# Delta rule in a four-stage fp32 kernel: keys multiply the state in the recurrence, the inverse's levels roll over the chunks, and the gate projections stand behind the inverse

## The chip, the cores and the metric

The kernel runs on one core of one Trainium2 chip. The metric is the device time of one execution in microseconds (us). All arithmetic is fp32.

## What is computed

Four layers follow each other over `BATCH = 8` sequences of `SEQ = 512` tokens with `DIM = 256` features: a gated mixer, a mixture of experts, a delta-rule attention and a token-selecting attention. The change is in the third one alone. Its reference, cut to what matters (8 heads, keys of 128, values of 64):

```
q = _causal_dw_conv_silu(x @ Wq, conv_q).reshape(bsz, seq_len, H, KD)
k = _causal_dw_conv_silu(x @ Wk, conv_k).reshape(bsz, seq_len, H, KD)
v = _causal_dw_conv_silu(x @ Wv, conv_v).reshape(bsz, seq_len, H, VD)
q = _l2norm(q)
k = _l2norm(k)
def step(state, inp):
    q_t, k_t, v_t, a_t, b_t = inp
    retained = jnp.einsum('bhvk,bhk->bhv', state, k_t)
    ...
    state = a4 * (state - b4 * rk) + b4 * vk
    o_t = jnp.einsum('bhvk,bhk->bhv', state, q_t)
    return (state, o_t)
...
gate = (x @ Wg).reshape(bsz, seq_len, H, VD)
rms = jax.lax.rsqrt(jnp.mean(out * out, axis=-1, keepdims=True) + EPS_RMS)
out = out * rms * o_norm_w * jax.nn.silu(gate)
return out.reshape(bsz, seq_len, VAL_DIM) @ Wo
```

The kernel computes the recurrence in `NC = 4` chunks of `C = 128` tokens. Within a chunk the dependence of each token on the earlier ones is a triangular matrix for each head; its inverse (`XT`) times the scaled values gives what each token adds to the state, and the state is carried from chunk to chunk.

## The kernel before

`stage_delta` writes the instructions of each engine out by hand; semaphores tie the engines together and no scheduler moves anything. Each engine has a function `body(pb, b)` that handles the front part of batch `b` (projections, convolutions, inverse, tail) and the recurrence and output of batch `pb = b - 1`. `body(None, 0)` and the last `body(7, None)` are written out; the seven between them are one hardware loop (`Fori`), so that every engine jumps back at its end.

One body goes through these parts, in this order on the tensor engine (PE):

- **K projections**: eight times `proj` (L1378, two 128x512 matmuls each). ScalarE copies each out (`cp`), multiplies it by a tap (`tap`), VectorE adds the three other taps (`conv(n)`, L1735: three instructions of 128x512), and ScalarE applies silu (`step`). There are 20 such convolutions in a batch: 0 to 7 keys, 8 to 11 values, 12 to 19 queries.
- **scan** of batch `pb`: four chunks; each multiplies the inverse by the values (L1392), a matrix `WT` by the state (L1396), the queries by the state (L1402), the keys by `Ud` for the next state (L1407) and `PQ` by `U` for the output (L1411). Each of these is a group of eight matmuls, one for each head. VectorE does `decay_state`, `decay_u`, `new_state`, `out_a` and `out_b` between the key convolutions and eight scans of the decays (`decay`, L1765).
- **gram**: the keys times themselves (L1422, four groups), multiplied by the decays on VectorE (`DG`, L1812); V projections; transposes of the keys (L1431); Q projections and the four gate projections (L1382).
- On VectorE alone meanwhile: 13 small instructions on the query norms, squares and sums of the output (L1820, L1821), the normalisation that ends in `yf`, and then the **base of the inverse** (L1838 to L1858), a chain of over 60 dependent instructions that inverts 32x32 blocks.
- **project_out** of batch `pb` (L1442, L1447) and on VectorE the residual add (L1863, `outr`), for which PE waits before the next part.
- **invert**: levels y5 (L1463), x5 (L1469), x11 (L1480), y6 (L1485), x6 (L1492) and then w (L1500), which multiplies the inverse by scaled keys into `WT`; all six for chunks 0 and 1, and then all six for chunks 2 and 3. VectorE scales y5 and y6 out of PSUM (L1872, L1880) and does the twelve convolutions 8 to 19 between them.
- **tail**: transposes of the values (L1509, scaled on VectorE at L1892, `values`), and four times the product of keys and queries (L1518) followed by sums of squared queries (L1523). The first L1518 waits until all 20 convolutions are through.

SyncE's queue loads weights, `hT`, decays (`ab`) and the residual input (`xin`, one body ahead), and stores the result.

## Time and profile before

| | us |
|---|---|
| median of three runs | 3805.78 |
| lowest and highest of them | 3804.8 and 3806.32 |
| the profiled execution, its own time | 3808.81 |
| its span, first to last instruction | 3806.2 |
| of it the delta stage, first K projection to its last store | 1713.2 to 3284.6 |
| of it the seven bodies of the loop | 1876.9 to 3187.7 |

Over the whole span PE is busy 86%, VectorE (DVE) 63%, ScalarE (ACT) 36%. PE's granted clock is shown as a share of 2.4 GHz: 0.50 is 1.2 GHz. In the delta stage no engine is busy all the time: the parts above follow each other, and in each another engine is the one that the others wait for.

### The profile page before, as it was taken

To read this page: it belongs to the slowest core of one execution; us is meant where nothing else is said; L and a number is where in the kernel's file an instruction comes from. 1 tells how busy PE (TensorE), PEld (TensorE's weight loads), DVE (VectorE), ACT (ScalarE), POOL (GpSimd) and SP (SyncE) were. 2 spreads that over 40 slices of the span, in tenths; PEclk is the share of its full clock that TensorE was granted. 3 is DMA by queue.
4 is the path that set the end of the run, shared out by engine and by line. 5 is a ranking of instruction groups with operands and counts; after the bars stand their busy time and mean duration, and the time that the engine had idled before them with its cause. 6 is when DMAs were issued, how large, how long until landed. Compare 5 with 4: busy or idle time off the path is not lost. (4 is left out here: it accounts for less than half of the span.)

```text
span 3806.2 us, 52445 instructions
## 1 busy us (share of the span) xinstructions
PE 3262.9 (86%) x18666; PEld 2525.1 (66%) x18666; DVE 2396.6 (63%) x5801; ACT 1356.5 (36%) x2713; POOL 158.4 (4%) x158
## 2 busy tenths in 40 slices
PE   5999938888999999747989898989898989488887
PEld 2665524445999999714867686868686869355554
DVE  6788425554777777766685858576767673354542
ACT  2333202221444444314534444444444442033232
POOL 0000000015111111000000000000000000000000
PEclk8999958999999999968797988888888886588786
DMA  1000080022899989741011111110111100100000
GB/s 62 23 17 12 11 160 12 11 75 81 305 322 317 320 318 323 253 152 64 34 34 35 34 36 34 35 34 35 34 35 34 35 20 1 53 12 23 12 17 12
DMA packets 203686, 327.31 MB, mean 86 GB/s; under 512 B 37449, under 2 KB 157522, under 8 KB 202258
## 3 DMA queue, kind: packets, MB, share of 16 engines
q1 hardware_dynamic: 196930, 305.94, 24.4%
q0 software_dynamic: 6480, 17.77, 1.2%
q8 instruction: 164, 2.69, 0.3%
q14 instruction: 112, 0.92, 0.1%
...
## 5 line engine op out<-in xcount | busy, mean ns | idle before, releaser
L767 PE MATMUL ex_ps<-ex_xbT,ex_w 128*128 128x128 f32 x4544 | 531.2, 275 | 1.7 <-DMA ex_b<-in_b_all_dram 1.2
L767 PEld LDWEIGHTS ex_ps<-ex_xbT,ex_w 128*128 128x128 f32 x4544 | 524.3, 192 | 6.1 <-DMA ex_b<-in_b_all_dram 1.8
L1378 PE MATMUL de_ps<-de_hT,de_w 128*128 128x512 f32 x640 | 306.2, 636 | 27.6 <-DMA de_w<-in_w_kqv_dram 13.9
L896 ACT ACTIVATE ex_t<-ex_ps,ex_b 128x128 f32<-128x128 f32 x568 | 208.8, 368 | 337.0 <-PE ex_ps L767 319.1
L1378 PEld LDWEIGHTS de_ps<-de_hT,de_w 128*128 128x128 f32 x640 | 129.0, 207 | 188.1 <-issue 186.0
L711 PE MATMUL ex_ps<-ex_xT,ex_w 128*128 128x512 f32 x512 | 230.6, 607 | 12.5 <-DVE ex_gl L1008 9.1
L1008 DVE SCALAR_TENSOR_TENSOR ex_gl<-ex_ps,ex_b,ex_t 128x128 f32<-128x128 f32 (+1 forms) x316 | 123.7, 391 | 137.3 <-ACT ex_t L896 69.4
L711 PEld LDWEIGHTS ex_ps<-ex_xT,ex_w 128*128 128x128 f32 x512 | 98.0, 195 | 131.8 <-issue 115.0
L1735 DVE SCALAR_TENSOR_TENSOR de_ya<-de_kx,de_taps,de_ya 128x512 f32<-128x512 f32 x192 | 142.5, 751 | 49.2 <-ACT de_ya L1574 44.7
L1008 DVE SCALAR_TENSOR_TENSOR ex_gm<-ex_ps,ex_b,ex_t 128x128 f32<-128x128 f32 (+1 forms) x316 | 121.8, 385 | 48.9 <-ACT ex_t L869 46.6
L177 PE MATMUL mx_ps<-mx_hT,mx_w_in 128*128 128x512 f32 x320 | 143.6, 605 | 8.3 <-ACT mx_hT L249 8.3
L1735 DVE SCALAR_TENSOR_TENSOR de_ya<-de_qx,de_taps,de_ya 128x512 f32<-128x512 f32 x192 | 142.9, 751 | 8.7 <-ACT de_ya L1574 2.6
L779 PE MATMUL ex_ps<-ex_w,ex_hid 128*128 128x256 f32 x568 | 134.5, 380 | 1.8 <-DVE ex_hid L1033 1.8
L1485 PE MATMUL de_ps<-de_PQ,de_DG 64*128 64x64 f32 x512 | 113.4, 419 | 15.7 <-ACT de_PQ L1638 15.7
L1485 PEld LDWEIGHTS de_ps<-de_PQ,de_DG 64*128 64x128 f32 x512 | 110.4, 329 | 19.6 <-ACT de_PQ L1638 19.6
L869 ACT ACTIVATE ex_t<-ex_ps,ex_b 128x512 f32<-128x512 f32 x64 | 44.0, 687 | 207.3 <-PE ex_ps L711 207.3
L177 PEld LDWEIGHTS mx_ps<-mx_hT,mx_w_in 128*128 128x128 f32 x320 | 60.7, 193 | 81.6 <-issue 67.4
L211 PE MATMUL mx_ps<-mx_h2T,mx_w_fc 128*128 128x512 f32 x256 | 113.7, 603 | 0.8 <-ACT mx_h2T L271 0.8
L1030 DVE SCALAR_TENSOR_TENSOR ex_gl<-ex_gl,ex_gm 128x128 f32<-128x128 f32 (+1 forms) x316 | 105.4, 333 | 11.1 <-DVE ex_gl L1028 0.2
L1033 DVE TENSOR_TENSOR ex_hid<-ex_gl,ex_gs 128x128 f32<-128x128 f32 (+1 forms) x316 | 105.0, 332 | 11.2 <-DVE ex_gl L1030 0.2
L220 PE MATMUL mx_ps<-mx_w_proj,mx_hid 128*128 128x256 f32 x512 | 111.8, 379 | 0.0
L779 PEld LDWEIGHTS ex_ps<-ex_w,ex_hid 128*128 128x128 f32 x568 | 102.5, 190 | 12.9 <-DVE ex_hid L1033 1.9
...
## 6 DMA issues: line engine op xcount, KB each, us to landing
...
ex_w<-in_w_all_dram SPq DMA_DIRECT2D x72, 512.0 KB, 8.6
...
ex_w<-ex_y_d SPq DMA_DIRECT2D x16, 512.0 KB, 6.1
mx_xin<-in_x_dram SPq DMA_DIRECT2D x8, 512.0 KB, 4.0
```

What stands on the lines that cost most here:

```text
L177: m = pe.matmul(ps[:, (n + 2) % 4, :], w_in[:, k, part * DIM + half * P:part * DIM + (half + 1) * P], hT[:, k, :], start=(k == 0), stop=(k ...
L211: m = pe.matmul(ps[:, 4 + f % 2, :], w_fc[:, k, f * P:(f + 1) * P], h2T[:, k, :], start=(k == 0), stop=(k == KT - 1))
L220: m = pe.matmul(ps[:, 6 + t // 2, t % 2 * DIM:(t % 2 + 1) * DIM], hid[:, f, t * P:(t + 1) * P], w_proj[:, f, :], start=(f == 0), stop=(f = ...
L711: m = pe.matmul(ps[:, bank, :], w[:, k, part * HID + c * P:part * HID + (c + 1) * P], xT[:, i % (LAG + 1), k, :], start=(k == 0), stop=(k ...
L767: m = pe.matmul(ps[:, n % 4, x * BLK:(x + 1) * BLK], w[:, k, part * HID + c * P:part * HID + (c + 1) * P], xbT[sx][:, k, :], start=(k == 0 ...
L779: m = pe.matmul(ps[:, 4 + sx, t * DIM:(t + 1) * DIM], hid[:, sx, c, t * P:(t + 1) * P], w2[s][:, c, :], start=(c == 0), stop=(c == HT - 1))
L896: act.activation(t1[:, n % 2, 0:BLK], ps[:, n % 4, 0:BLK], ACT.Identity, bias=b13[s][:, 0, n:n + 1]).then_inc(t1_ready, 1)
L1008: dve.scalar_tensor_tensor(out=out[:, 0:width], in0=in0, scalar=b3[:, 1, n:n + 1], in1=t1[:, n % 2, 0:width], op0=ALU.add, op1=ALU.mult).t ...
L1030: link2(dve.scalar_tensor_tensor(out=gl[:, 0:width], in0=gl[:, 0:width], scalar=1.0, in1=gm[:, 0:width], op0=ALU.add, op1=ALU.mult))
L1378: m = pe.matmul(ps[:, n % 2, :], w[:, g % SLOTS, k, n % 2 * P:(n % 2 + 1) * P], hT[:, k, :], start=(k == 0), stop=(k == KT - 1))
L1485: m = pe.matmul(ps[:, 2 + c % 2, hd * HALF:(hd + 1) * HALF], DG[0:HALF, c, hd, :], X11[0:HALF, c % 2, hd, :], start=True, stop=True, skip_ ...
L1735: m = dve.scalar_tensor_tensor(out=ya[:, n % 3, :], in0=xp(n)[:, i:i + SEQ], scalar=taps[:, col_of(n), i:i + 1], in1=ya[:, n % 3, :], op0= ...
```

## The change

- `WT`, its matmuls (L1500) and the scaled keys are gone. In the recurrence the keys multiply the state (`with_state`), VectorE scales the product and adds it to the values (`add_state`, two instructions), and only then does the inverse multiply the values (`u_products`). Chunk 0 of a batch has no state and skips these.
- V projections and the four gram groups stand between the groups of the scan. On VectorE the convolutions, decays and gram products are ordered to match.
- The squares of the output are ScalarE's, the small instructions on the query norms stand at the start of VectorE's body.
- The levels of the inverse roll over the four chunks.
- The gate projections follow the inverse, ahead of the tail.
- `xin` shares memory with `o` and is loaded when `o` has been transposed; `Xc` shares memory with the values and is cleared by GpSimd in each body; keys are double buffered.
- The hardware loop is written out (`for pb, b in steps`).

```diff
-        WT = DG
-        kcg = sb("kcg", [P, 2, H, C])
+        kx = sb("kx", [P, 2, H, PADW])
+        KV = sb("KV", [P, H, V])
+        Xc = vb[:, :, :, :].rearrange("p c h v -> p (c h) v")
+        xin = o[:, 0:2, :, :].rearrange("p c h v -> p (c h v)").rearrange("p (t d) -> p t d", d=DIM)
+        gram = lambda c: 0 if c % 2 == 0 else 6
+        steps = [(b - 1 if b else None, b if b < BATCH else None) for b in range(BATCH + 1)]
...
+                    sp.wait_ge(s["oTp"], pb * VTL + VTL)
+                    sp.dma_start(xin[:, :, :], x_in[pb].rearrange("(t p) d -> p t d", p=P)).then_inc(s["x_ld"], 16)
...
+            def scan(pb, b):
+                def u_products(c):
                     for hd in range(H):
+                        m = pe.matmul(ps[:, 2, hd * V:(hd + 1) * V], XT[:, c, hd, :], vb[:, c, hd, :], start=True, stop=True, skip_group_check=True)
+                    m.then_inc(s["up"], 1)
+
+                def with_state(c):
+                    pe.wait_ge(s["st"], pb * (NC - 1) + c)
                     for hd in range(H):
+                        m = pe.matmul(ps[:, 3, hd * V:(hd + 1) * V], kc(pb, hd, c), ST[:, hd, :], start=True, stop=True, skip_group_check=True)
+                    m.then_inc(s["ks"], 1)
+                    pe.wait_ge(s["od"], pb * NC + c)
                     for hd in range(H):
                         m = pe.matmul(ps[:, 4, hd * V:(hd + 1) * V], qc(hd, c), ST[:, hd, :], start=True, stop=True, skip_group_check=True)
                     m.then_inc(s["qs"], 1)
+                    pe.wait_ge(s["vs"], pb * (NC - 1) + c)
+
+                def state_step(c):
+                    pe.wait_ge(s["ud"], pb * (NC - 1) + c + 1)
+                    for hd in range(H):
+                        m = pe.matmul(ps[:, 3, hd * V:(hd + 1) * V], kt[:, c, hd, :], Ud[:, hd, :], start=True, stop=True, skip_group_check=True)
+                    m.then_inc(s["su"], 1)
+
+                def outputs(c):
                     pe.wait_ge(s["u"], pb * NC + c + 1)
                     for hd in range(H):
                         m = pe.matmul(ps[:, 5, hd * V:(hd + 1) * V], PQ[:, c, hd, :], U[:, hd, :], start=True, stop=True, skip_group_check=True)
                     m.then_inc(s["os"], 1)
 
...
+                pe.wait_ge(s["pq"], pb * NC + NC)
+                pe.wait_ge(s["vbr"], pb * NC + NC)
+                u_products(0)
+                value(0)
+                state_step(0), outputs(0)
+                value(1)
+                with_state(1), u_products(1)
+                value(2)
+                state_step(1), outputs(1)
+                value(3)
+                with_state(2), u_products(2)
+                if b is not None:
+                    gram_kk(pb, b, 0)
+                state_step(2), outputs(2)
+                if b is not None:
+                    gram_kk(pb, b, 1)
+                with_state(3), u_products(3)
+                if b is not None:
+                    gram_kk(pb, b, 2)
+                outputs(3)
+                if b is not None:
+                    gram_kk(pb, b, 3)
...
-                    for c in both:
-                        pe.wait_ge(s["x6"], b * NC + c + 1)
-                        pe.wait_ge(s["kcg"], b * NC + c + 1)
-                        bank = 6 if c % 2 == 0 else 2
-                        for hd in range(H):
-                            m = pe.matmul(wide(bank)[:, hd, :], kcg[:, c % 2, hd, :], XT[:, c, hd, :], start=True, stop=True, skip_group_check=True)
-                        m.then_inc(s["wp"], 1)
+                pe.wait_ge(s["xc"], b + 1)
+                y5(0), y5(1), x5(0), y5(2), x5(1), y5(3)
+                x11(0), x5(2), x11(1), y6(0), x5(3), x11(2), y6(1)
+                x6(0), x11(3), y6(2), x6(1), y6(3), x6(2), x6(3)
...
+                    for n in range(Q0, G0):
                         proj(b, n, pb is None)
                 if pb is not None:
                     project_out(pb, b)
                 if b is not None:
                     invert(pb, b)
+                    for n in range(G0, PROJ):
+                        proj(b, n, pb is None)
                     tail(b)
...
-            body(None, 0)
-            with pe.Fori(0, BATCH - 1) as pb:
-                body(pb, pb + 1)
-            body(BATCH - 1, None)
+            for pb, b in steps:
+                body(pb, b)
...
+                    x5(0), x5(1)
+                    step(8, CONV - 1)
+                    x11(0), x5(2), x11(1)
+                    step(9, CONV - 1)
+                    x5(3), x11(2)
+                    step(10, CONV - 1)
+                    x6(0), x11(3)
+                    step(11, CONV - 1)
+                    x6(1)
+                    step(12, CONV - 1)
+                    x6(2), x6(3)
+                    for n in range(G0, PROJ):
+                        cp(n)
+                    for n in range(13, CONV):
                         step(n, CONV - 1)
...
+                def squares(t):
+                    if not first:
+                        act.wait_ge(s["od"], pb * NC + t + 1)
+                        act.wait_ge(s["os"], pb * NC + (2 if t < 2 else NC))
+                        act.activation(squared(t), o[:, t, :, :].rearrange("p h v -> p (h v)"), ACT.Square).then_inc(s["sqo"], 1)
...
+                def add_state(c):
+                    dve.wait_ge(s["ks"], pb * (NC - 1) + c)
+                    dve.wait_ge(s["scl"], pb + 1)
+                    cB(dve.tensor_tensor(KV[:, :, :], heads(3), over_v(ncg[:, pb % 2, c, :]), ALU.mult))
+                    dve.tensor_tensor(vb[:, c, :, :], vb[:, c, :, :], KV[:, :, :], ALU.add).then_inc(s["vs"], 1)
...
+                        for n in range(6):
+                            conv(n)
+                        dve.wait_ge(s["cl_ld"], 32 * pb + 32)
+                        decay_u(0)
+                        conv(6)
+                        first_state()
+                        conv(7)
+                        first_out()
+                        decay_state(1)
+                        dve.wait_ge(s["ab_ld"], 16 * b + 16)
+                        decay(0, 1)
+                        add_state(1)
+                        decay(1, 2)
+                        out_a(1)
+                        decay_u(1)
+                        decay(2, 4)
+                        new_state(1)
+                        decay(4, 5)
+                        out_b(1)
+                        decay_state(2)
+                        decay(5, 6)
+                        add_state(2)
+                        decay(6, 7)
+                        out_a(2)
+                        decay_u(2)
+                        decay(7, H)
+                        decayed_gram(0)
+                        new_state(2)
+                        out_b(2)
+                        sum_squares(0), sum_squares(1)
+                        decayed_gram(1)
+                        add_state(3)
+                        out_a(3)
+                        decayed_gram(2)
+                        out_b(3)
+                        cB.end()
+                        decayed_gram(3)
+                        sum_squares(2), sum_squares(3)
+                        normalise()
...
+                    y5(0), y5(1)
+                    conv(8)
+                    y5(2)
+                    conv(9)
+                    y5(3)
+                    conv(10)
+                    y6(0)
+                    conv(11)
+                    y6(1)
+                    conv(12)
+                    y6(2), y6(3)
+                    conv(13)
+                    values(0), values(1)
+                    conv(14)
+                    values(2), values(3)
+                    for n in range(15, CONV):
+                        conv(n)
```

How this stands in the instruction streams, first on PE in the first body, from the base of the inverse to the end of the value transposes. Names are outputs and inputs; `x8` counts instructions. Before:

```order
L1378 MATMUL de_ps<-de_hT,de_w 128x512 x16
L1382 MATMUL de_ps<-de_w_g,de_hT 128x512 x8
L1463 MATMUL de_ps<-de_Xc,de_DG 128x64 x16
L1469 MATMUL de_ps<-de_PQ,de_Y 64x32 x16
L1480 MATMUL de_ps<-de_ident,de_XT 64x64 x16
L1485 MATMUL de_ps<-de_PQ,de_DG 128x64 x16
L1492 MATMUL de_ps<-de_XT,de_PQ 64x64 x16
L1500 MATMUL de_ps<-de_XT,de_kcg 128x128 x16
```

and the end of the same stretch in the change:

```order
L1513 MATMUL de_ps<-de_PQ,de_DG 128x64 x8
L1494 MATMUL de_ps<-de_PQ,de_Y 64x32 x8
L1504 MATMUL de_ps<-de_ident,de_XT 64x64 x8
L1513 MATMUL de_ps<-de_PQ,de_DG 128x64 x8
L1523 MATMUL de_ps<-de_XT,de_PQ 64x64 x8
L1504 MATMUL de_ps<-de_ident,de_XT 64x64 x8
L1513 MATMUL de_ps<-de_PQ,de_DG 128x64 x8
L1523 MATMUL de_ps<-de_XT,de_PQ 64x64 x8
L1513 MATMUL de_ps<-de_PQ,de_DG 128x64 x8
L1523 MATMUL de_ps<-de_XT,de_PQ 64x64 x16
L1380 MATMUL de_ps<-de_w_g,de_hT 128x512 x8
L1543 MATMUL de_ps<-de_ident,de_vx 128x128 x16
```

The levels alternate between chunks, no 128x128 product of w stands behind them, and the eight gate matmuls moved from ahead of the inverse to between its last level and the value transposes.

On VectorE in the same body, from the end of the base. Before (x9 is three convolutions):

```order
L1858 STREAM_TRANSPOSE de_PQ<-de_PQ 128x32x32
L1872 TENSOR_TENSOR de_Y<-de_ps,de_scT 32x8x32 x4
L1735 SCALAR_TENSOR_TENSOR de_ya<-de_vx,de_taps,de_ya 128x512 x9
L1880 TENSOR_TENSOR de_PQ<-de_ps,de_scT 64x512 x2
L1735 SCALAR_TENSOR_TENSOR de_ya<-de_vx,de_taps,de_ya 128x512 x3
L1735 SCALAR_TENSOR_TENSOR de_ya<-de_qx,de_taps,de_ya 128x512 x6
L1872 TENSOR_TENSOR de_Y<-de_ps,de_scT 32x8x32 x4
L1735 SCALAR_TENSOR_TENSOR de_ya<-de_qx,de_taps,de_ya 128x512 x9
L1880 TENSOR_TENSOR de_PQ<-de_ps,de_scT 64x512 x2
L1735 SCALAR_TENSOR_TENSOR de_ya<-de_qx,de_taps,de_ya 128x512 x9
L1892 TENSOR_TENSOR de_vb<-de_ps,de_scT 128x512 x4
```

and the second half of it in the change:

```order
L1959 TENSOR_TENSOR de_PQ<-de_ps,de_scT 64x512
L1769 SCALAR_TENSOR_TENSOR de_ya<-de_vx,de_taps,de_ya 128x512 x3
L1959 TENSOR_TENSOR de_PQ<-de_ps,de_scT 64x512
L1769 SCALAR_TENSOR_TENSOR de_ya<-de_qx,de_taps,de_ya 128x512 x3
L1959 TENSOR_TENSOR de_PQ<-de_ps,de_scT 64x512 x2
L1769 SCALAR_TENSOR_TENSOR de_ya<-de_qx,de_taps,de_ya 128x512 x3
L1964 TENSOR_TENSOR de_vb<-de_ps,de_scT 128x512 x2
L1769 SCALAR_TENSOR_TENSOR de_ya<-de_qx,de_taps,de_ya 128x512 x3
L1964 TENSOR_TENSOR de_vb<-de_ps,de_scT 128x512 x2
L1769 SCALAR_TENSOR_TENSOR de_ya<-de_qx,de_taps,de_ya 128x512 x15
```

Before, all twelve convolutions stand ahead of the scaling of the values (`de_vb`); now convolution 14 stands behind the first two of them, and 15 to 19 behind all four.

On PE in the scan of a later body, one chunk (chunk 1 to the outputs of it). Before:

```order
L1392 MATMUL de_ps<-de_vb,de_XT 128x64 x8
L1394 REGISTER_ALU
L1396 MATMUL de_ps<-de_oT,de_DG 128x64 x8
L1402 MATMUL de_ps<-de_oT,de_qx 128x64 x8
L1405 REGISTER_ALU
L1407 MATMUL de_ps<-de_oT,de_kt 128x64 x8
L1411 MATMUL de_ps<-de_oT,de_PQ 128x64 x8
```

and in the change:

```order
L1392 MATMUL de_ps<-de_oT,de_kx 128x64 x8
L1396 MATMUL de_ps<-de_oT,de_qx 128x64 x8
L1386 MATMUL de_ps<-de_vb,de_XT 128x64 x8
L1376 MATMUL de_ps<-de_hT,de_w 128x512 x2
L1403 MATMUL de_ps<-de_oT,de_kt 128x64 x8
L1409 MATMUL de_ps<-de_oT,de_PQ 128x64 x8
```

The product with the inverse (`de_vb,de_XT`) moved behind the two with the state, and a projection stands between it and the state's own step.

## Rows read from the trace of the kernel before

**Rows 1.** Busy PE, PEld, DVE, ACT, POOL in the loop; granted clock, DMA share, GB/s:

```profile
1876.90:3187.70 1310.80, 1180.40 (x7282) 966.59 (x7281) 919.05 (x1687) 579.93 (x1050) 0.00 (x0) 0.86 0.10 34
```

**Rows 2.** Timeline of PE at two turns of bodies; start, length, then instruction:

```profile
1876.90 13.98 PE L1378 MATMUL de_ps<-de_hT,de_w 128*128 128x512 f32 x32
...
2247.39 1.84 PE L1523 MATMUL de_ps<-de_ones,de_ya 128*128 128x1 f32 x16
2250.99 16.96 PE L1378 MATMUL de_ps<-de_hT,de_w 128*128 128x512 f32 x32 [1.75 <-issue]
```

**Rows 3.** Timeline of DVE: convolution 4, start of the base, residual add:

```profile
2269.74 2.33 DVE L1735 SCALAR_TENSOR_TENSOR de_ya<-de_kx,de_taps,de_ya 128x512 f32<-128x512 f32 x3 [1.10 <-ACT de_ya L1574]
...
2328.52 2.08 DVE L1838 STREAM_TRANSPOSE de_PQ<-de_PQ 128x1024 f32<-128x1024 f32 x1
...
2364.42 1.22 DVE L1863 TENSOR_TENSOR de_xin<-de_xin,de_ps 128x1024 f32<-128x1024 f32 x1 [1.65 <-PE de_ps L1447]
```

**Rows 4.** Groups of DVE by line in the loop: busy us, mean ns:

```profile
L1735 DVE SCALAR_TENSOR_TENSOR de_ya<-de_qx,de_taps,de_ya 128x512 f32<-128x512 f32 x168 | 125.0, 751 | 7.7 <-ACT de_ya L1574 2.3
...
L1765 DVE TENSOR_TENSOR_SCAN de_ab<-de_ab,de_ident 128x512 f32<-128x512 f32 x56 | 64.6, 1206 | 0.0
...
L1756 DVE TENSOR_TENSOR de_o<-de_ps,de_g 128x512 f32<-128x512 f32 x28 | 19.2, 686 | 12.1 <-PE de_ps L1402 12.1
```

**Rows 5.** Timeline of the scan: two PE groups, and DVE's wait for the first:

```profile
2278.74 1.95 PE L1396 MATMUL de_ps<-de_oT,de_DG 128*128 128x64 f32 x16
2280.52 1.95 PE L1402 MATMUL de_ps<-de_oT,de_qx 128*128 128x64 f32 x16
...
2280.72 0.69 DVE L1747 TENSOR_TENSOR de_oT<-de_ps,de_ae 128x512 f32<-128x512 f32 x1 [0.54 <-PE de_ps L1396]
```

**Rows 6.** Timeline of PE, inverse of the first body, chunks 0 and 1:

```profile
1801.27 7.06 PE L1463 MATMUL de_ps<-de_Xc,de_DG 128*128 128x64 f32 x32 [7.77 <-ACT de_Xc L1620]
1808.26 3.62 PE L1469 MATMUL de_ps<-de_PQ,de_Y 128*64 128x32 f32 x32
1811.81 2.04 PE L1480 MATMUL de_ps<-de_ident,de_XT 64*64 64x64 f32 x16
1814.61 7.09 PE L1485 MATMUL de_ps<-de_PQ,de_DG 64*128 64x64 f32 x32 [0.76 <-ACT de_PQ L1638]
1821.63 3.67 PE L1492 MATMUL de_ps<-de_XT,de_PQ 64*64 64x64 f32 x32
```

**Rows 7.** The same columns as Rows 1, four stretches:

```profile
1805.00:1825.00 20.00, 19.24 (x128) 18.54 (x127) 12.18 (x19) 7.18 (x14) 0.00 (x0) 0.50 0.00 1
...
2250.00:2256.00 6.00, 5.01 (x6) 2.17 (x7) 0.38 (x1) 0.60 (x1) 0.00 (x0) 0.51 0.89 339
2268.00:2300.00 32.00, 31.86 (x284) 31.59 (x283) 27.72 (x36) 8.94 (x15) 0.00 (x0) 1.00 0.03 9
...
3190.00:3250.00 60.00, 60.00 (x284) 60.00 (x283) 9.90 (x15) 2.39 (x4) 0.00 (x0) 0.50 0.00 1
```

**Rows 8.** Timeline, one loop body: start of the inverse, values, first L1518:

```profile
2178.24 3.78 PE L1463 MATMUL de_ps<-de_Xc,de_DG 128*128 128x64 f32 x32 [1.63 <-DVE de_xin L1863]
...
2231.94 1.29 DVE L1892 TENSOR_TENSOR de_vb<-de_ps,de_scT 128x512 f32<-128x512 f32 x2 [1.96 <-PE de_ps L1509]
...
2234.81 2.02 PE L1518 MATMUL de_ps<-de_qx,de_kx 128*128 128x128 f32 x16 [0.87 <-DVE de_vb L1892]
```

**Rows 9.** Timeline of PE, two grams of the first body after an idle stretch:

```profile
1741.48 5.49 PE L1422 MATMUL de_ps<-de_kx 128*128 128x128 f32 x32 [11.55 <-ACT de_kx L1578]
```

**Rows 10.** Timeline of DVE, start of the base in the first body:

```profile
1766.69 2.05 DVE L1838 STREAM_TRANSPOSE de_PQ<-de_PQ 128x1024 f32<-128x1024 f32 x1 [8.94 <-ACT de_PQ L1602]
```

**Rows 11.** Timeline, last body: end of the scan, start of project_out:

```profile
3251.91 0.69 DVE L1761 TENSOR_TENSOR de_o<-de_o,de_ps 128x512 f32<-128x512 f32 x1 [2.72 <-PE de_ps L1411]
...
3269.39 3.77 PE L1442 MATMUL de_ps<-de_ident,de_o 128*128 128x128 f32 x16 [17.51 <-DVE de_o L1830]
```

**Rows 12.** DMA issues by line: size, us to landing:

```profile
de_xin<-x_d SPq DMA_DIRECT2D x8, 512.0 KB, 3.9
```

407 lines of the change are left out of this document (179 added, 228 removed).

## The prediction

> **What bounds the kernel now.** I read the page first (PE 86% busy, DVE 63%, so the ends of chains matter and not a full engine), then the busy time by stage: the change is all in the delta stage, whose seven loop bodies take 1310.8 us, 187.3 each, with PE busy 90% but at a mean granted clock of 0.86 [rows 1]. Then I followed one body through the timelines of PE, ACT and DVE, asking at each part who is waited for. From the first K projection on PE (2250.99) [rows 2]:
> - to convolution 4 (2269.74 [rows 3]): 18.75 us. PE is slow here: 16.96 us for eight projections, against 13.98 at 1876.90, where no gap stands before them [rows 2]; the clock was 0.51 in this stretch [rows 7]. The 1.75 us gap before it is the jump of the loop. So a turn costs 1.75 + 2.98 = 4.7 us.
> - convolution 4 to the base of the inverse (2328.52): 58.8 us, all on DVE. The base ends at 2364.42 - 1.65 = 2362.77 (the residual add stood idle 1.65 us for PE's project_out) [rows 3], so it takes 34.25 us. 1.22 us of add and the start of y5 follow: y5 starts about 37.4 us after the base began.
> - y5 to the first L1518 (2178.24 to 2234.81, another body): 56.6 us [rows 8]; then four rounds of L1518 and L1523 to the end of PE's body, 2247.39 + 1.84 = 2249.23: 14.4 us [rows 2]. Sum: 1.75 + 18.75 + 58.8 + 37.4 + 71.0 = 187.7, which is the body.
>
> **Part 1, the turn.** Writing the loop out removes the 1.75 us gap, and the K projections then follow the tail as at 1876.90, without the slow start: 15.8 us to convolution 4 instead of 18.75. That is 4.7 us in six turns. If the clock falls all the same it is 1.75.
>
> **Part 2, scan and gram.** One product with the inverse replaces two products, and DVE gets `add_state`. Units: a group of eight 128x64 matmuls is followed by the next after 1.78 us and seen by DVE after 1.98 (2278.74, 2280.52, 2280.72) [rows 5]; a convolution is three times 0.751, a decay scan 1.15 to 1.2, a 128x512 DVE operation 0.60 in a row and 0.69 alone [rows 4]; a projection 13.98 / 8 = 1.75 [rows 2]. In the new order, counted from convolution 4, DVE reaches `decay_u(0)` at 4.5, `first_state` at 7.4, and after that it is a chain with PE for each chunk: keys by state (2.0), `add_state` (1.4), queries by state and then inverse by values (seen 3.6 after the keys' product), `decay_u` (0.7), a projection or gram that PE does first (1.8), state step (2.0), `new_state` (0.7). I get `add_state` at 12.7, 25.1 and 37.7, `new_state(1)` and `(2)` at 19.8 and 32.3, the last outputs at 45, the last `DG` at 47.9, two sums 1.2, 15 small instructions 3.4, two times four products 5.0: the base starts at 57.5. Before it was 58.8: decays and DG products that stood in a row now fill the waits, 2.9 us of small instructions went to the start of the body, where DVE waits for the first tap, and 2.6 us of squares went to ACT; what is won is nearly all spent on the longer chain. **Gain 1.3 us.** Bounds: 0, and 5.5 if DVE never waited longer than now.
>
> **Part 3, up to y5.** Without the gate projections (4 x 1.75 = 7.0 us) project_out is through ahead of the base's end, so y5 starts 34.25 + 1.4 = 35.7 us after the base began: **gain 1.7 us.** The input, loaded only after the transposes of `o`, lands in 3.9 us [rows 12], during the 16 matmuls of project_out and what is left of the base; without this cover it would cost its 3.9. GpSimd's clearing of `Xc` has the whole base as cover.
>
> But PE now stands idle for 1.65 + 7.0 - 1.7, some 7 to 10 us, before y5. In the first body it also stands idle, 7.77 us, and there y5 ran 7.06 us, x5 3.62, and the clock was 0.50 from then on (1805 to 1825) [rows 6, 7]; in the loop, with 1.63 us of idle, two y5 groups take 3.78 [rows 8]. I take the first body's rows for every body.
>
> **Part 4, the inverse.** By [rows 6] one chunk costs y5 3.50, x5 1.78, x11 0.95, y6 3.51, x6 1.80. Four chunks are 46.2 us of PE, and in the rolling order I find no wait of PE on another engine. w is gone, which is what makes this shorter than the present 53 us. DVE however runs dry. From y5's start, DVE has: y5(0) 3.7, y5(1) 7.2, convolution 8 to 10.4, y5(2) not before 12.5, convolution 9 to 15.7, y5(3) 17.8, convolution 10 to 21.0, y6(0) 25.1, convolution 11 to 28.1, y6(1) 31.4, convolution 12 to 34.4, y6(2) 37.7, y6(3) 43.0, convolution 13 to 46.0. It has waited some 20 us and done six convolutions; six are left.
>
> **Part 5, the gates behind it.** The next DVE instruction, `values(0)`, waits for value transposes that stand behind four gate projections on PE. These start at 46.2 at half clock: 4 x 1.75, and 2.98 more as in [rows 2], so 56.2. Queued behind `values(0)` on DVE are convolutions 14 to 19, and for them wait ACT's silu and PE's L1518. So: values 0 and 1 (0.7 after PE, 1.25 long) to 58.0, convolution 14 to 60.2, values 2 and 3 to 61.5, five convolutions of 2.27 to 72.8, silu and semaphores 0.8: L1518 starts at 73.6 instead of 56.6. **Loss 17.0 us.** Bounds: with the inverse as slow but the gates as cheap as nothing, 7; with PE at full clock all through, see the rival.
>
> **Part 6, the tail.** Before L1518 PE has been idle for some 14 us. After such a gap two groups of 128x128 took 5.49 us, against 3.6 at full clock [rows 9]: 1.9 lost. Whether the clock is up again when L1523 comes between them, no row shows: its first pair at half clock costs another 1.7 (it is a chain of weight loads like y5's, which doubled). I take 3.4 in all. Bounds: 1.7, and 13.3 if all four rounds stay at half clock; then the next K projections start slow too (3.0).
>
> **Sum.** A body: 15.8 + 57.5 + 35.7 + 73.6 + 14.4 + 3.4 = 200.4 us. Seven are 1402.8, against 1310.8 [rows 1]: +92.0. First body: here DVE waited 8.94 us for ACT's diagonals, which stood behind copies of V projections on ACT [rows 10]; these now come first, and 6.3 of it goes. Its inverse is at half clock already; from y5 to K it took 1876.90 - 1801.27 = 75.6, and is to take 91.4: +15.8 - 6.3 = +9.5. Last body: 17 groups instead of 19 at 3.41 us (60 us at clock 0.50 [rows 7]), and three to four waits of 1 us more: -2.2. From its last outputs to project_out it took 3269.39 - 3251.91 = 17.5 us [rows 11]; small instructions and squares off the path leave 11.8: -5.7. In all +93.6: 3808.8 becomes 3902.4. The profiled execution stands 3.0 us above the median of the runs, so I say **3899 us** for the median, 2.5% slower.
>
> **The rivals.**
> - *Full clock in the inverse: faster.* At full clock y5 takes 1.89 [rows 8], and the scan, with the same 128x64 groups, ran at clock 1.00 for 32 us [rows 7]. If y6 and x6 halved too, PE would be through in 46.2 / 2 = 23 us; then DVE decides: y5 and y6 6.3, six convolutions 13.6, perhaps 5 of waits, 25; gates to 32, values 1.3 and six convolutions 14.9: L1518 at about 50, no loss in the tail. A body takes 15.8 + 57.5 + 35.7 + 50 + 14.4 = 173.4, 13.9 less than now; with 17.5 less in the first body and 7.9 in the last the median is about 3683. With y6 and x6 at half clock, as in [rows 6], and y5 and x5 at full, PE is through at 37, L1518 comes at 61, and the median is about 3774. It decides when y5 starts at clock 1.00 and stays there. Against it: the last body's 60 us of the same groups, without a pause, at 0.50 [rows 7]. Chance 0.15.
> - *All rounds of the tail cold.* 9.9 us more in eight bodies and 3.0 in seven: about 3999. For it: the scan of the last body, which came straight behind a tail, ran at 0.50 for 60 us [rows 7]. Against: the two groups of [rows 9], in which the clock rose. Chance 0.13.
> - *My chain in the scan is too pessimistic, or convolutions slip less.* 5 us a body less than I say, and only the first gram slow: about 3850. Chance 0.17, the forecast itself 0.50.
> - *It comes out even*: gains of the turn and the scan as large as the loss. Each us at L1518 counts eight times, so that needs it at 65 and no loss in the tail, which is the case if the clock rises halfway through the inverse. Chance 0.05.
>
> The Trainium skill, page "TensorE: Matmul & The Clock Gate", Part 1, says that activity releases the throttle, so that a PE that works without pause runs at 2.4 GHz. By that rule the first rival holds, since in the rolling order PE hardly waits. Here the 60 us at 0.50 in the last body speak against it, with no idle in them, and so do 20 us in the first.
>
> **Numbers.** A measurement of this kernel can tell about 0.2% (7.6 us) from no change. The range goes from 3820 (between the even case and the third rival) to 3965 (between forecast and the cold tail): it leaves out the first rival and most of the second. Faster: the first rival and a bit of the even case, 0.17; same 0.03; slower 0.80.
>
> **What would show it.** In the profile after: K projections in some 14 us without a gap before them; base starting 57 to 58 us after convolution 4; y5 35.7 after that; two y5 groups in 7.0 us and clock 0.50 from there to the gates; a wait of DVE of 10 us or more ahead of `values(0)`, released by PE's value transposes; L1518 73 us after y5. I am wrong if the clock is high in the inverse, or if DVE does not wait ahead of the values.

## The result and the profile after

| | kernel before | changed kernel |
|---|---|---|
| median | 3805.29 | 4004.39 |
| lowest and highest | 3803.1 and 3806.32 | 3996.55 and 4015.7 |
| profiled execution, its span | | 4010.0, 4008.2 |

The ratio is 1.0526, with a 95% interval of 1.0497 to 1.0556: 5.3% slower, where 2.5% was forecast, and outside the range. The profiled run stands 107.6 us above the 3902.4 that the sum gave for it.

The tensor engine's timeline around one turn of bodies (start, length, instruction, idle time before it and who ended it), tail, K projections and the first groups of the scan, which answer to [rows 2, 5]:

```profile
2078.34 3.78 PE L1552 MATMUL de_ps<-de_qx,de_kx 128*128 128x128 f32 x16 [14.62 <-ACT de_qx L1614]
2081.91 3.41 PE L1557 MATMUL de_ps<-de_ones,de_ya 128*128 128x1 f32 x16
...
2105.67 16.49 PE L1376 MATMUL de_ps<-de_hT,de_w 128*128 128x512 f32 x32
...
2129.17 3.68 PE L1403 MATMUL de_ps<-de_oT,de_kt 128*128 128x64 f32 x16 [3.51 <-DVE de_oT L1781]
2132.64 3.62 PE L1409 MATMUL de_ps<-de_oT,de_PQ 128*128 128x64 f32 x16
```

VectorE in the same body: convolutions 4 and 5, `decay_u(0)` (L1781), the first instruction of `add_state(1)` (L1795), the base, and the wait ahead of the values, which answer to [rows 3, 8]:

```profile
2123.95 4.56 DVE L1769 SCALAR_TENSOR_TENSOR de_ya<-de_kx,de_taps,de_ya 128x512 f32<-128x512 f32 x6 [1.11 <-ACT de_ya L1610]
2128.43 0.68 DVE L1781 TENSOR_TENSOR de_oT<-de_ps,de_ae 128x512 f32<-128x512 f32 x1
...
2140.74 0.69 DVE L1795 TENSOR_TENSOR de_KV<-de_ps,de_ncg 128x512 f32<-128x512 f32 x1 [1.58 <-PE de_ps L1392]
...
2185.36 2.10 DVE L1917 STREAM_TRANSPOSE de_PQ<-de_PQ 128x1024 f32<-128x1024 f32 x1
...
2276.82 1.29 DVE L1964 TENSOR_TENSOR de_vb<-de_ps,de_scT 128x512 f32<-128x512 f32 x2 [9.93 <-PE de_ps L1543]
```

The tensor engine from y5 to the next tail:

```profile
2220.58 7.06 PE L1485 MATMUL de_ps<-de_vb,de_DG 128*128 128x64 f32 x32 [13.79 <-DVE de_o L1942]
...
2267.34 9.01 PE L1380 MATMUL de_ps<-de_w_g,de_hT 128*128 128x512 f32 x16
...
2293.45 3.78 PE L1552 MATMUL de_ps<-de_qx,de_kx 128*128 128x128 f32 x16 [14.62 <-ACT de_qx L1614]
```

And the granted clock in four stretches (columns as in [rows 1]): a tail, K projections, the inverse, the next tail:

```profile
2078.34:2105.67 27.33, 27.33 (x129) 27.33 (x129) 4.90 (x4) 4.82 (x8) 0.00 (x0) 0.50 0.02 10
2105.67:2122.30 16.63, 16.63 (x37) 7.41 (x37) 10.95 (x26) 7.65 (x14) 0.00 (x0) 0.85 0.43 161
2220.58:2267.34 46.76, 46.76 (x288) 45.16 (x289) 19.70 (x30) 16.36 (x29) 0.00 (x0) 0.50 0.04 12
2293.45:2320.80 27.35, 27.35 (x129) 27.35 (x129) 4.90 (x4) 4.82 (x8) 0.00 (x0) 0.50 0.04 17
```

Put together, one body (2105.67 to 2320.77), each time from the start of one row to the next:

| step | predicted | measured |
|---|---|---|
| K projections to convolution 4 | 15.8 | 18.3 |
| convolution 4 to the base | 57.5 | 61.4 |
| base to y5 | 35.7 | 35.2 |
| y5 to the first L1552 (was L1518) | 73.6 | 72.9 |
| tail | 17.8 | 27.3 |
| sum | 200.4 | 215.1 |

Seven times 14.7 us are 103 of the 107.6. The tail alone is 9.5 of a body: it runs at clock 0.50 from its first row to its last, in eight of eight bodies.

### The profile page after: what moved, and what is told of

Same layout as the page of the kernel before. It is cut to its first block and busy times, and to the rows that moved or that the text cites. A ratio compares the mean times of both kernels' runs of the same rounds, so it can differ in the third digit from the quotient of the medians.

```text
span 4008.2 us, 48416 instructions
## 1 busy us (share of the span) xinstructions
PE 3331.6 (83%) x17898; PEld 2592.1 (65%) x17898; DVE 2392.4 (60%) x5793; ACT 1273.5 (32%) x2457; POOL 173.5 (4%) x165
## 5 line engine op out<-in xcount | busy, mean ns | idle before, releaser
L1552 PE MATMUL de_ps<-de_qx,de_kx 128*128 128x128 f32 x512 | 120.5, 430 | 117.0 <-ACT de_qx L1614 117.0
L1485 PE MATMUL de_ps<-de_vb,de_DG 128*128 128x64 f32 x512 | 115.3, 423 | 112.8 <-DVE de_o L1942 96.6
L1552 PEld LDWEIGHTS de_ps<-de_qx,de_kx 128*128 128x128 f32 x512 | 112.7, 332 | 118.9 <-ACT de_qx L1614 118.9
L1485 PEld LDWEIGHTS de_ps<-de_vb,de_DG 128*128 128x128 f32 x512 | 111.0, 331 | 117.3 <-issue 116.2
L1769 DVE SCALAR_TENSOR_TENSOR de_ya<-de_kx,de_taps,de_ya 128x512 f32<-128x512 f32 x192 | 141.9, 750 | 56.6 <-ACT de_ya L1610 52.1
L1987 DVE TENSOR_TENSOR de_PQ<-de_ps,de_ab 128x1024 f32<-128x1024 f32 x32 | 39.2, 1225 | 169.9 <-PE de_ps L1552 169.9
L1513 PE MATMUL de_ps<-de_PQ,de_DG 64*128 64x64 f32 x512 | 116.1, 418 | 0.0
L1513 PEld LDWEIGHTS de_ps<-de_PQ,de_DG 64*128 64x128 f32 x512 | 112.6, 329 | 0.9
L1557 PEld LDWEIGHTS de_ps<-de_ones,de_ya 128*128 128x128 f32 x512 | 113.1, 333 | 0.0
```

The lines of the kernel that those rows point to most:

```text
L1485: m = pe.matmul(ps[:, 2 + c % 2, hd * HALF:(hd + 1) * HALF], DG[:, c, hd, :], Xc[:, c * H + hd, :], start=True, stop=True, skip_group_chec ...
L1513: m = pe.matmul(ps[:, 2 + c % 2, hd * HALF:(hd + 1) * HALF], DG[0:HALF, c, hd, :], X11[0:HALF, c % 2, hd, :], start=True, stop=True, skip_ ...
L1552: m = pe.matmul(wide(pair(c))[:, hd, :], kc(b, hd, c), qc(hd, c), start=True, stop=True, skip_group_check=True)
L1769: m = dve.scalar_tensor_tensor(out=ya[:, n % 3, :], in0=xp(b, n)[:, i:i + SEQ], scalar=taps[:, col_of(n), i:i + 1], in1=ya[:, n % 3, :], o ...
```

## The experiments

Up to four figures are given for each, in us, from the timelines of the profiled execution: y5 to the first product of keys and queries, tail, K projections, and end of the tail to the next y5 ("scan and base"). A tail reads 0.1 us longer when it is taken to the end of its last row and not to the next one, so 27.3 and 27.4 are the same tail. The changed kernel has 72.9, 27.3, 16.4 to 16.8, 114.7; the kernel before had 56.6, 14.4, 16.7 to 17.0 and 116.7. Ratios are to the kernel before, run beside each. F(n) stands for n matmuls of `w_g[:, 0, 0:P]` by `w_g[:, 1, :]`, 128x512, into a free PSUM bank; nobody reads them.

**The turn alone.** The kernel before, loop written out.

```diff
-            with pe.Fori(0, BATCH - 1) as pb:
-                body(pb, pb + 1)
+            for pb in [None] + list(range(BATCH)):
+                body(pb, 0 if pb is None else (pb + 1 if pb + 1 < BATCH else None))
```

> The kernel before, with only the hardware loop of the delta stage written out. My reading: a turn of the loop costs a 1.75 us gap on PE and 2.98 us of K projections at half clock, in six turns, so 28 us less than before: about 3777, with eight K projections in some 14 us in every body. Rival: the clock falls after the tail whether there is a gap or not (the tail's 128x1 groups do it), then only the gap goes: about 3795. Second rival: the longer instruction stream costs as much as it saves: 3805.

Measured 3777.77 us, ratio 0.994 (0.992 to 0.9961). K takes 14.0 in all bodies. That is 26 us below the kernel before in the same comparison (3803.96), against 28 from Part 1's 4.7 us a turn. The agreement is in part luck: body for body, two are some 7 us shorter than before, and in the last four PE stands idle 3.2 us ahead of y5 instead of 1.6, y5 starts at half clock, the first product comes after 60.4 instead of 56.6, and these bodies gain 1.5 to 3.6 us. The changed kernel does not get warm K projections, because its tail is cold.

**Fill before the tail.**

```diff
+                F(16)
                 pe.wait_ge(s["act"], b * CONV + CONV)
```

> The changed kernel with 16 extra 128x512 matmuls on PE (13.8 us at full clock, into a PSUM bank that nobody reads then) where it waits for the last convolution, ahead of L1552. They add no dependence. My reading: PE's 14.6 us of idle there drop the clock, and the tail (27.3 us against 14.4), the K projections (16.5 against 13.9) and the first groups of the scan pay for it. With the idle filled, the tail takes 14.4 and the rest follows: 12.9 x 8 + 3 x 7 + 3 x 7 = 145 us less, about 3860. Rival: the alternation of L1552 and L1557 lets the clock fall anyway, after one or two rounds: about 3950. If the clock is not the cause: 4004.

Measured 3890.65 us, ratio 1.0235 (1.0216 to 1.0255). Tail 14.4 and K 14.0 in all bodies, y5 to product unchanged at 72.5 to 73.7. So with PE's idle time ahead of the tail filled, nothing in the tail makes it cold. The gain is 114 us, not 145: scan and base only went from 114.7 to between 111.3 and 113.0. The wait of 3.51 for L1783 (`decay_u(0)`) is still there with a warm K, and the groups behind it are at half clock:

```profile
2096.00 2.99 PE L1403 MATMUL de_ps<-de_oT,de_kt 128*128 128x64 f32 x16 [3.51 <-DVE de_oT L1783]
2098.78 3.62 PE L1409 MATMUL de_ps<-de_oT,de_PQ 128*128 128x64 f32 x16
```

**Fill before the inverse.**

```diff
                 pe.wait_ge(s["ktr"], b * NC + NC)
+                F(15)
                 if pb is not None:
                     pe.wait_ge(s["outr"], pb + 1)
```

> The changed kernel with 15 extra 128x512 matmuls (12.9 us) on PE between project_out and the inverse, where it is idle 13.8 us. Reading A: PE enters the inverse at full clock and falls back during the small groups, as the loop bodies of before did some 7 us after the start: the first y5 groups take 1.9 instead of 3.5, worth about 5 us in each of eight bodies, about 3965. Reading B, the rival of the prediction: the clock stays up once it is up, the inverse takes 23 to 37 us instead of 46, and DVE waits less ahead of each level: about 3860 or less.

Measured 3915.68 us, ratio 1.0274 (1.0229 to 1.0319). y5 to product falls to 60.6 to 62.2 in five bodies and to about 70 in two; the first body stays at 71.5. The clock falls inside the inverse, as reading A had it and as the next run shows, but what the warm start brings is some 11 us in most bodies and not 5. Two of the eight tails took 16.3 and 16.5 us, though PE stood idle for the same 14.62 us ahead of them as ahead of the six at 27.3.

**Both fills.**

> The changed kernel with PE's idle time ahead of y5 and ahead of the tail both filled with matmuls of 128x512 whose results nobody reads (15 and 16). Theory A (each fill works in its own stretch): the gain of the fill before the tail, 114 us, and of the earlier first product, 8 us in each of 8 bodies: about 3828. Theory B (a warm tail leads to a cold inverse all the same): 3890, as with the second fill alone.

Measured 3814.8 us, ratio 1.0024 (1.0014 to 1.0034). The gains nearly add: 113.7 and 88.7 us for each fill alone, 189.6 for both. One inverse of it, PE's rows and then the granted clock of two stretches:

```profile
2178.66 3.79 PE L1485 MATMUL de_ps<-de_vb,de_DG 128*128 128x64 f32 x32 [0.83 <-DVE de_o L1946]
...
2190.41 2.10 PE L1513 MATMUL de_ps<-de_PQ,de_DG 64*128 64x64 f32 x16
2192.44 1.91 PE L1494 MATMUL de_ps<-de_PQ,de_Y 128*64 128x32 f32 x16
2194.28 1.06 PE L1504 MATMUL de_ps<-de_ident,de_XT 64*64 64x64 f32 x8
2195.14 3.62 PE L1513 MATMUL de_ps<-de_PQ,de_DG 64*128 64x64 f32 x16
```

```profile
2178.66:2190.40 11.74, 11.74 (x128) 11.33 (x129) 8.42 (x15) 7.12 (x12) 0.00 (x0) 1.00 0.14 47
2192.44:2214.07 21.63, 21.63 (x145) 20.86 (x145) 9.54 (x13) 7.20 (x14) 0.00 (x0) 0.50 0.00 1
```

Behind the 0.83 us ahead of y5 no row has a pause in front of it, and the same L1513 group takes 2.10 and then 3.62. The narrow products of the inverse do not hold the full clock by themselves. That does not go for every narrow product: the scan's 128x64 groups ran at 1.00 for 32 us behind the K projections, and at 0.50 for 60 us behind a tail [rows 7]. Which of the inverse's groups loses the clock was not tried. The Trainium skill, page "TensorE: Matmul & The Clock Gate", Part 1, says that activity releases the throttle; here PE was active without a gap and the clock fell. In the kernel before, y6 is at half clock in each half too, there behind pauses of up to 1.8 us; w is wide, and behind it y5 is at full clock again (no run put w back to test this):

```profile
2187.22 7.08 PE L1485 MATMUL de_ps<-de_PQ,de_DG 64*128 64x64 f32 x32 [1.39 <-ACT de_PQ L1638]
...
2197.84 5.98 PE L1500 MATMUL de_ps<-de_XT,de_kcg 128*128 128x128 f32 x32
2204.93 3.79 PE L1463 MATMUL de_ps<-de_Xc,de_DG 128*128 128x64 f32 x32 [1.11 <-ACT de_DG L1646]
```

**Sums last.** All L1557 products (128x1, two heads to each row above) behind the four L1552 groups, instead of between them.

> The changed kernel with the four groups of sums of squared queries behind the four products of keys and queries instead of between them. Theory A (in the tail it is the sums, 128x1 matmuls between the products, that keep the clock at 0.50; four 128x128 groups in a row let it rise as two gram groups of the first body did): first product 3.8 us, the others about 2, tail 16 to 17 us, K warm: about 3915. Theory B (the idle time ahead decides alone): tail stays at 27 us, about 4004.

Measured 3953.29 us, ratio 1.0393 (1.0375 to 1.041). Tail 21.2. The products no longer stay at half clock (there they took 15.1 us), but the sums lose part of it again (four rows of 3.41 are 13.6 us at half clock, four of 1.84 are 7.4 at full):

```profile
2276.01 9.91 PE L1552 MATMUL de_ps<-de_qx,de_kx 128*128 128x128 f32 x64 [14.62 <-ACT de_qx L1614]
2285.76 11.50 PE L1557 MATMUL de_ps<-de_ones,de_ya 128*128 128x1 f32 x64
```

So in the changed kernel both are needed for a tail at half clock from end to end: the idle time ahead, and the one-column products between. They do not suffice, as the next run shows.

**Gates back** ahead of `project_out`, on PE and ACT.

> The changed kernel with the four gate projections (and ScalarE's copies of them) back ahead of project_out; all else as changed. My reading: the value transposes then follow the inverse at once, values(0) comes at 46.9 instead of 56.7 us after y5, and L1552 at 64 instead of 73: 9 us less in eight bodies, about 3932; the tail stays at half clock, since PE still idles over 10 us ahead of it. Rival: the gates' place does not matter because the six convolutions behind them bound the stretch either way: 4004.

Measured 3855.87 us, ratio 1.0129 (1.0094 to 1.0164). y5 to product is 64.8, as worked out (64); what was not foreseen is that the tails then are 15.9 to 16.6 in six of eight bodies. PE stands idle for 14.16 us ahead of each of the eight, and their instructions are those of the changed kernel: the first group of 128x128 is at half clock, and in six of them the clock is up behind it, as the forecast assumed for all. That is why the time is 3856 and not 3932.

**Convolutions first.** Gates where the change has them, VectorE's order changed (and ACT's to match).

```diff
-                    y6(2), y6(3)
-                    conv(13)
-                    values(0), values(1)
-                    conv(14)
-                    values(2), values(3)
-                    for n in range(15, CONV):
-                        conv(n)
+                    y6(2)
+                    conv(13)
+                    y6(3)
+                    for n in range(14, CONV):
+                        conv(n)
+                    for c in range(NC):
+                        values(c)
```

> The changed kernel with VectorE's convolutions 14 to 19 ahead of the four scalings of the values, y6 of chunk 3 behind convolution 13, and ScalarE's silus between its copies of the gates. Same work, other order. Theory A (the gates behind the inverse cost only because VectorE stands behind the values while six convolutions are left; the cold tail and the slow K projections follow from PE's idle time ahead of the tail): VectorE works while PE does the gates, the first product of keys and queries comes some 60.5 us after y5 instead of 73, PE is idle some 3 us ahead of it, the tail takes about 14.4 us and K 14.0: 28 us less in a body, about 3765 to 3785. Theory B (the queue costs, but the tail is at half clock whatever stands ahead): 12.5 us a body, about 3904.

Measured 3862.41 us, ratio 1.0155 (1.0136 to 1.0174), 80 to 100 us more than expected, but 142 us less than the changed kernel, by order alone. y5 to product 65.3, not 60.5 (VectorE waits 3.1 us for ACT's tap behind the gate copies, and the last transposes wait for it); tail 16.3 in all bodies, its first group at half clock, not 14.4; K 14.0. The profiled execution took 3847.8, the others up to 3869.8.

**Both of the last two.**

> The changed kernel with the gate projections ahead of project_out, as before the change, and VectorE's convolutions 14 to 19 ahead of the values. Theory A (the order on VectorE is what counts, the gates behind the inverse are then a useful cover): VectorE is through some 60 us after y5 in either place of the gates, but PE is idle 9 to 10 us ahead of the tail, so that the tail is cold at its start in all bodies and all through in some: 3800 to 3840, slower than the version with the gates behind. Theory B (gates behind the inverse are bad in any order): as fast as or faster than that version.

The profiled execution took 3815.92 us, with y5 to product 61.8 and tails 16.0 to 16.4; the three others took 3869.95 to 3911.68. The ratio, 1.023 (1.0178 to 1.0281), is that of the three; the profiled execution is 0.3% above the kernel before (3806.14). Inconclusive as to the order: the same instructions lie 96 us apart, and their mean granted clock with them (0.839 in the first, 0.815 in the longest). Only the fastest has a timeline.

**Queries inside the inverse.** On top of convolutions first.

```diff
-                y5(0), y5(1), x5(0), y5(2), x5(1), y5(3)
-                x11(0), x5(2), x11(1), y6(0), x5(3), x11(2), y6(1)
-                x6(0), x11(3), y6(2), x6(1), y6(3), x6(2), x6(3)
+                y5(0), y5(1), query(14), x5(0), y5(2), query(15), x5(1), y5(3)
+                x11(0), x5(2), query(16), x11(1), y6(0), x5(3), query(17), x11(2), y6(1)
+                x6(0), query(18), x11(3), y6(2), x6(1), query(19), y6(3), x6(2), x6(3)
```

> The changed kernel with VectorE's convolutions ahead of the values (as in the run of that order alone), and six of the eight query projections moved from ahead of project_out into the inverse, one between every three to five groups of its levels. No work is added. Theory A (the 64-column products of the inverse lose the clock on their own, and 128x512 products between them give it back, as the w groups did before the change): y5 starts at half clock, from the first projection on most groups take half the time, PE is through with inverse and gates some 45 us after y5, VectorE decides, the first product of keys and queries comes at about 52 us instead of 65: about 3755. Theory B (once y5 has started cold, the clock stays at 0.50 until the inverse is through): PE needs 47 plus 15 plus 9 us, the first product comes at about 76: about 3950.

Measured 3872.29 us, ratio 1.0178 (1.0161 to 1.0195). Theory A's clock, not its time:

```profile
2185.81 7.06 PE L1485 MATMUL de_ps<-de_vb,de_DG 128*128 128x64 f32 x32 [24.05 <-DVE de_o L1946]
2192.66 3.36 PE L1376 MATMUL de_ps<-de_hT,de_w 128*128 128x512 f32 x4
2195.96 1.12 PE L1494 MATMUL de_ps<-de_PQ,de_Y 128*64 128x32 f32 x16
2197.01 2.00 PE L1485 MATMUL de_ps<-de_vb,de_DG 128*128 128x64 f32 x16
...
2215.94 3.68 PE L1376 MATMUL de_ps<-de_hT,de_w 128*128 128x512 f32 x4
```

Behind one projection the clock was back (1.00 from 2195.96 to 2215.94), where the changed kernel, without it, stayed at 0.50. But the first, fifth and sixth of the six take 3.4 to 3.7 us here instead of 1.75; the fifth and sixth are at half clock themselves, with groups at full clock on both sides. With 10.5 us more work in it (six times 1.75), the inverse takes 45.3 us, and the first product comes after 59.8 to 63.9 instead of 65.3. What that wins is lost again in the tails: four of eight are at 27.4, the others at 15.8 to 16.3.

**Fill before the inverse with convolutions first.**

> The changed kernel with convolutions ahead of the values, and 15 matmuls of 128x512 whose result nobody reads behind project_out, in PE's idle time ahead of y5. Theory A (the two gains add): first product 10 us earlier than with the order alone in most bodies, 55 us after y5: about 3782. Theory B (VectorE with its twelve convolutions is the limit at 60 us or more): about 3825.

Measured 3818.96 us, ratio 1.0047 (1.0028 to 1.0066). y5 to product is 52.8 or 53.9 behind the first body (63.7), but every second tail is 27.4. One of its six executions took 3901.03, the others 3812.15 to 3836.21.

**Recurrence order** on top of it.

```diff
-                        for n in range(6):
+                        for n in range(4):
                             conv(n)
                         dve.wait_ge(s["cl_ld"], 32 * pb + 32)
                         decay_u(0)
+                        conv(4)
+                        first_state()
+                        conv(5)
+                        first_out()
+                        decay_state(1)
                         conv(6)
-                        first_state()
+                        add_state(1)
                         conv(7)
-                        first_out()
-                        decay_state(1)
...
```

The decays and later waits follow in the new order too, and ScalarE's copy of the same product (`u(0)`) moves up, ahead of two silus.

> As the run with fill and order, and in the recurrence VectorE's decay_u(0) stands behind convolution 3 instead of 5, and the convolutions 4 to 7 fill the waits of chunk 0 instead of two decay scans. PE then has no wait of 3.5 us behind the first product with the inverse. Theory A (that wait, with the half clock behind it, is why the base starts 61.4 us after convolution 4 and not 57.5): base 3 to 4 us earlier in each of seven bodies, 21 to 28 us less than the run without it, about 3757. Theory B (VectorE's own work decides there): the same time as without it.

Measured 3768.68 us, ratio 0.991 (0.9893 to 0.9927). Scan and base 106.9 and 108.0 instead of 113.1 and 115.4; that is 50 us in all, twice what theory A expected. Two of its tails, the last transposes and first rows of each:

```profile
2218.98 1.97 PE L1545 MATMUL de_ps<-de_ident,de_vx 128*128 128x128 f32 x8 [5.59 <-DVE de_vb L1970]
...
2225.32 3.41 PE L1559 MATMUL de_ps<-de_ones,de_ya 128*128 128x1 f32 x16
...
2408.28 1.97 PE L1545 MATMUL de_ps<-de_ident,de_vx 128*128 128x128 f32 x8 [5.07 <-DVE de_vb L1970]
...
2414.62 2.02 PE L1559 MATMUL de_ps<-de_ones,de_ya 128*128 128x1 f32 x16
```

With 5.59 us of idle time ahead of the last transposes the tail takes 27.4, with 5.07 it takes 16.3, in four bodies each. It is not a threshold: a tail of "queries inside the inverse" took 15.8 behind 5.59.

**Recurrence order alone**, on the changed kernel.

> The changed kernel with nothing but VectorE's order in the recurrence: decay_u(0) behind convolution 3, convolutions 4 to 7 in the waits of chunk 0, decays later. Theory A (PE's wait of 3.5 us for decay_u(0) is what made the base start late): the stretch from convolution 4 to the base is 5 to 7 us shorter in seven bodies, about 4004 - 42 = 3962. Theory B (it only helps where K is warm): less than half of that, 3985 or more.

Measured 3952.12 us, ratio 1.0392 (1.0375 to 1.0409). Scan and base fell from 114.7 to 107.7 in seven bodies, and the wait ahead of L1403 is gone. The first of its tails took 16.4, behind the same idle time as the other seven at 27.3:

```profile
1863.58 3.78 PE L1552 MATMUL de_ps<-de_qx,de_kx 128*128 128x128 f32 x16 [14.62 <-ACT de_qx L1614]
1867.15 2.20 PE L1557 MATMUL de_ps<-de_ones,de_ya 128*128 128x1 f32 x16
```

**Paced queries.** Convolutions first and recurrence order; six query projections behind `project_out`, each waiting for a count of the base's chain.

```diff
+                    for n, reached in zip(range(Q0 + 2, G0), (0, 44, 52, 60, 70, 82)):
+                        if reached:
+                            pe.wait_ge(s["dvC"], b * (20 + 2 * (Q - 2) + 2) + reached)
+                        proj(b, n, pb is None)
```

> The changed kernel with convolutions ahead of the values and the recurrence order, no matmul added: six of the eight query projections stand behind project_out, each waiting for a further point in VectorE's base, so that PE's one idle stretch of 13.5 us ahead of y5 becomes six of 2 to 3 us. Theory A (only a long pause loses the clock): y5 starts at full clock as with the fill, about 3769. Theory B (short pauses lose it as well, or the work between is too little): two y5 groups take 7 us, the first product comes 65 us after y5, about 3862 - 40 = 3822.

Measured 3902.76 us, ratio 1.0221 (1.0154 to 1.0288). The clock held for four pieces and then fell, with 1.0 to 2.8 us between them:

```profile
2175.01 1.98 PE L1376 MATMUL de_ps<-de_hT,de_w 128*128 128x512 f32 x4 [1.52 <-DVE de_PQ L1945]
...
2185.98 3.78 PE L1376 MATMUL de_ps<-de_hT,de_w 128*128 128x512 f32 x4 [1.01 <-DVE de_PQ L1945]
2192.68 7.06 PE L1485 MATMUL de_ps<-de_vb,de_DG 128*128 128x64 f32 x32 [2.92 <-ACT de_vb L1652]
```

Short pauses with wide work between them did not save y5, and all eight tails were at 27.4.

**Fill inside the tail**, F(10) between the value transposes of chunks 1 and 2, on top of fill, order and recurrence order.

> As the run with fill, order and recurrence order, and in the tail ten matmuls of 128x512 with no reader between the value transposes of chunk 1 and those of chunk 2, where PE was idle 5.1 to 5.6 us in each body. Theory A (that idle time is what makes the tail start at half clock, and in four of eight bodies stay there): tail 14.4 us and K 14.0 in all bodies, which is 13.9 us in four bodies and 1.9 in four, about 3769 - 63 = 3706. Theory B (it depends on what PE did in the inverse before, not on this wait): four tails stay at 27 us, about 3760.

Measured 3725.23 us, ratio 0.9791 (0.9774 to 0.9807). Tail 14.4 and K 14.0 in all bodies. The fill is longer than the wait (8.75 us for ten, against 5.1 to 5.6), so the product came 1 to 4 us later. With F(6):

> As the run with ten matmuls between the value transposes, with six: a matmul of 128x512 took 0.87 us there, so ten are 8.7 us in a wait of 5.1 to 5.6, and six are 5.2. Theory A (the tail stays warm, the surplus goes): first product 1 to 2.5 us earlier in eight bodies, about 3713. Theory B (the shorter stretch is not enough and some tails fall to half clock): about 3740.

Measured 3705.06 us, ratio 0.975 (0.9723 to 0.9777), product at 51.8 to 53.2 in six bodies, 62.6 in the first and 61.4 in the last; tails 14.4 in all.

**Gates inside the inverse**, one behind each of x5(2), x5(3), x6(0) and x6(1), with F(18) in the tail.

> As the run with fill, order and recurrence order, with the four gate projections between the later levels of the inverse instead of behind it, and eighteen matmuls without a reader between the value transposes of the tail. Theory A (wide products in the inverse keep the clock, so that PE is through in 23 + 7 us and VectorE decides): all groups of the inverse at full clock, first product about 47 us after y5 instead of 53, warm tails: about 3706 - 48 = 3658. Theory B (VectorE's convolutions already decide at 53): as the run with the fill inside the tail, about 3706.

Measured 3737.38 us, ratio 0.9825 (0.9804 to 0.9846). y5 to product is 55.8 to 59.8 behind the first body. In the body from 2161.45 all narrow groups but the last few were at full clock, but three of the four gate projections took 3.5 to 3.7 us, so that PE was through after 38.8 us and not 30. The fill lasted until 2219.20 and VectorE waited 6.62 us for the transposes behind it. With F(11):

> As the run with the gates inside the inverse, with eleven matmuls in the tail instead of eighteen, whose 15.7 us outlasted VectorE by 6.6. Theory A (that surplus hid the gain of the placement): first product 55 us after y5 instead of 58 to 60, about 3737 - 8 x 4 = 3705. Theory B (the projections between the levels cost as much as the clock they hold gives back, VectorE decides in any case): as the other run of this call, within 8 us.

Measured 3695.43 us, ratio 0.9713 (0.9697 to 0.9729), product 48.3 to 53.8 after y5 in the seven later bodies, 9.6 us below the F(6) version; the executions of the two overlap (3688.17 to 3700.37, and 3699.11 to 3718.63). This is the fastest version found: 2.9% below the kernel before. Its gain over the changed kernel, 309 us, is all order and clock; it computes more than the changed kernel does.

## Why the prediction was wrong

*Part 1, the turn*: in the kernel before, writing the loop out was worth what was said (3803.96 to 3777.77, 26 us or 4.4 a turn for six), though by gains and losses that were not in the sum. The condition "follow the tail as at 1876.90" did not hold, since the tail was cold: K took 16.4 to 16.8, and convolution 4 came 2.5 us late.

*Part 2, scan and gram*: said 57.5, came 61.4. VectorE reached `decay_u(0)` at 4.5, as said (2128.43 against 2123.95). The terms that were mis-sized are PE's behind it: PE waited 3.51 us there, the next two groups took some 3.45 us each instead of 1.8, and `add_state(1)` came at 16.8 instead of 12.7; of the 4.1 us, 3.9 were left at the base. The groups behind the wait ran at half clock also with a warm K. The new order of the recurrence (`decay_u(0)` and `u(0)` up, convolutions 4 to 7 in chunk 0's waits) was worth 52 us by itself; its moves were not tried one by one. That the longer chain eats the gains was right; the sign was not (58.8 before, 61.4 after).

*Parts 3 to 5* held: y5 after 35.2 (35.7), two groups in 7.06, inverse 46.8 (46.2), a wait of 9.93 ahead of the values released by L1543, product at 72.9 (73.6). PE's idle time ahead of y5 was 13.8 us and not "some 7 to 10". With the gates back the product came at 64.8 (64). The cause given was only half of it. I made the idle time before y5 answerable for the clock all through. It answers for the first 12 us; after that the clock falls by itself, and the change had taken away the w groups behind which it had been up again. The [rows 8] show y5 at 3.78 us, and I stopped there: the y6 group of the same body, at 7.08, stood four rows further down.

*Part 6, the tail*, is the step that failed. It took 3.4 us for a cold start, by [rows 9], and the cost was 12.9 in every body. In [rows 9] two groups of 128x128 follow each other; here 128x1 products stand between them. With the sums moved last the clock does come up in the products. The forecast's case, a clock that is up again behind the first group, does occur: in six tails of eight with the gates back (14.16 us of idle time ahead), and behind the very same 14.62 us in one with the recurrence order alone and in two with the fill before the inverse. So the size of the step is shown, and that the idle time ahead is needed for it; why the clock stayed down in all eight tails here is open. The bound of 13.3 and the second rival (all rounds cold, 3999) describe what came, 4004. That the scan of the last body ran at half clock for 60 us behind a tail was the better row. The tail's 9.5 us over the forecast, the 2.5 of K behind it and Part 2's 3.9 are 15.9 of a body; 1.2 came back in Parts 3 to 5.

*First and last body*: from y5 to K 100.8 us against 91.4, again the tail; y5 itself 12.0 us earlier than before, of which 5.2 is the stage's earlier start (1708.0 against 1713.2), which was not followed up, and 6.3 the diagonals, as said (VectorE waited 2.61 us for them instead of 8.94). The last body was 7.6 us shorter up to project_out, as said (7.9), although the -2.2 in it does not follow from its terms: two groups less and three to four waits more make -2.8 to -3.8.

*The change as a whole*: its parts are not all losses. With the waits that it opened closed, the same recurrence, rolling levels and late gates give 3705 us, and 3695 with the gates inside the inverse. Both versions compute fills that nobody reads, which none of the forecast's cases had. The rival "faster" named the right lever, a full clock in the inverse, but the inverse does not keep it without wide work. Its second case (y5 and x5 at full clock, y6 and x6 at half, product at 61) is near what the fill before the inverse gave: 60.6 to 62.2 in five bodies.

Not settled: what makes tails warm or cold where their rows differ by half a microsecond of idle time or not at all, and why executions of one kernel differed by 96 us. The runs show that the time goes with the clock, not which event tips it.
